# A second attention whose scores rotate over three PSUM banks and whose exponentials run in halves

## The chip, the cores and the metric

The kernel runs on one core of a Trainium2 chip. A core has five engines with queues of their own, which meet only at semaphores: TensorE (PE, its weight loads PEld), VectorE (DVE), ScalarE (ACT), GpSimd (POOL) and SyncE (SP). TensorE writes its results to PSUM, eight banks of 128 partitions by 512 floats; VectorE and ScalarE read them there. The metric is the device time of one launch in microseconds, the median of several runs.

## The reference

A small language model on 16 sequences of 128 tokens: embedding with a decaying memory and four MLP layers, a fast weight attention, a mixture of experts, then a second attention and a second mixture. The change touches the second attention alone:

```python
def _L1_attn_ref(x, Wqk, Wv, Wpos, bpos, Wproj, bproj, gating):    # x: (16, 128, 64), 8 heads of 8
    qk = (x @ Wqk.T).reshape(Bb, Nn, 2, Hh, hd)
    q = qk[:, :, 0].transpose(0, 2, 1, 3)
    k = qk[:, :, 1].transpose(0, 2, 1, 3)
    patch_score = softmax(einsum('bhnd,bhmd->bhnm', q, k) * hd ** (-0.5))
    pos_score = softmax((rel @ Wpos.T + bpos).transpose(2, 0, 1))
    g = sigmoid(gating)[None, :, None, None]
    attn = (1.0 - g) * patch_score + g * pos_score[None]
    attn = attn / attn.sum(axis=-1, keepdims=True)
    v = (x @ Wv.T).reshape(Bb, Nn, Hh, hd).transpose(0, 2, 1, 3)
    out = einsum('bhnm,bhmd->bhnd', attn, v).transpose(0, 2, 1, 3).reshape(Bb, Nn, Cc)
    return out @ Wproj.T + bproj
h = h + _L1_attn_ref(_layernorm(h), ...)
h = h + _L1_ffn_ref(_layernorm(h), ...)
```

## The kernel before

Each engine has one program, written out by hand in the order in which it runs, and counts on named semaphores. The word token stands here for one of the T = 16 sequences (128 positions on the partitions); CH = 4 tokens make a chunk, and there are NC = 4 chunks. In the second attention a token's eight heads give scores of 128 x 1024, in two halves of four heads, 512 columns each, one PSUM bank a half. The semaphores are `s_mm0` and `s_mm1` (scores of a half), `s_sub` (maximum subtracted, two per token), `s_exp` (exponential), `s_T` (transposed, two per token), `p_ready` (copied to SBUF, two per token), `av_mm` (values multiplied).

TensorE, for each token t: `scores(t + 1)` (lines 1759 to 1772, sixteen products of 64 rows, into banks 2 and 3), after both halves of token t have been subtracted; at odd t `values_back` (line 1806); `values(t - 1)` (line 1793); side work by the place j of the token in its chunk: j = 0 `turn_input` of the next chunk (line 1816) and, in odd chunks, `positional` (line 1840); j = 1 `project_qk` (lines 1825 and 1826); j = 3 `turn_attended` (line 1850) and `project_v` (line 1831); then `turn_scores(t)` (line 1781, eight transposes into banks 4 and 5); at j = 3 `project_out` (line 1856).

VectorE, for each token: `normalise(t)` (lines 2488 to 2499), for each half the maximum out of PSUM (line 2494) and the subtraction from PSUM to the SBUF tile `sexp` (line 2498); behind it side work: layer norms (lines 409 to 424), `mix` (lines 2508 to 2515), `add_attended` (line 2521).

ScalarE, for each token: `take_turned(t - 1)`, two copies of 512 columns from banks 4 and 5 to `pexp` (line 1226); one exponential over the token's 1024 columns in `sexp` (line 1243); side work: j = 0 `save_values_T` (line 1218) and `take_x` (line 1185), in odd chunks `take_positions` (line 1210); j = 1 two query copies (line 1190) and the keys (line 1195) of the next chunk; j = 2 `save_values_T` and the other two query copies; j = 3 `take_attended` (line 1204) and `take_values` (line 1199).

`sexp` and `pexp` hold two tokens each. Scores of the first token of a chunk wait for that chunk's four query copies. Behind the last token TensorE goes on with `turn_x` (line 1640) for the second mixture of experts. GpSimd works out the layer norms' factors (lines 391 to 402) and adds to `H`; no DMA runs in this stretch.

Of the kernel before, what the change touches and what calls it, by code (L numbers as in the profile page):

```python
# [6 lines left out]
ACT = mybir.ActivationFunctionType  # L7
# [5 lines left out]
P = 128  # L13


T = 16
# [3 lines left out]
D = 64  # L20
# [3 lines left out]
HD = D // NH  # L24
# [114 lines left out]
def build(nc, a):  # L139
# [9 lines left out]
    with ExitStack() as ctx:  # L149
        def sb(name, shape, dt=F32):  # L150
            return ctx.enter_context(nc.sbuf_tensor(name, shape, dt))
# [4 lines left out]
        bank = [ctx.enter_context(nc.psum_tensor(f"bank{i}", [P, 512], F32)) for i in range(8)]  # L156
# [4 lines left out]
        ident = sb("ident", [P, P])  # L161
# [108 lines left out]
        sexp = KKf[:, 0:2048].rearrange("p (k h n) -> p k h n", k=2, h=NH)  # L270
        pexp = UVf[:, 4608:6656].rearrange("p (k h n) -> p k h n", k=2, h=NH)
# [94 lines left out]
        def turn_bank(k, c):  # L366

            return bank[6 if k == 0 else 2 + c if c < 2 else c % 2]

        def expert_bank(k, c, e):  # L370

# [511 lines left out]
        def _(act):  # L883
# [313 lines left out]
            def take_values(c):  # L1197
                act.wait_ge(s["d_v"], c + 1)
                act.activation(vaug[c % 2][:, :, :, 0:HD], bank[1][:, 0:CH * D].rearrange("p (t h d) -> p t h d", t=CH, h=NH),
                               ACT.Copy).then_inc(s["d_vcopy"], 1)  # L1200
# [16 lines left out]
                    act.wait_ge(s["av_back"], p - 1)  # L1217
                act.activation(avT[:, p % 2, :], bank[6][:], ACT.Copy).then_inc(s["av_saved"], 1)

            def take_turned(t):  # L1220

                for g in range(2):
                    act.wait_ge(s["s_T"], 2 * t + g + 1)
                    if t >= 2:
                        act.wait_ge(s["av_mm"], t - 1)
                    act.activation(pexp[:, t % 2, 4 * g:4 * g + 4, :].rearrange("p h n -> p (h n)"), bank[4 + g][:],
                                   ACT.Copy).then_inc(s["p_ready"], 1)

            save_sums(2)
            take_x(0)  # L1230
# [4 lines left out]
            take_values(0)  # L1235
            for t in range(T):
                c, j = divmod(t, CH)
                if t:
                    take_turned(t - 1)
                if t == T - 1:  # L1240
                    take_attended(NC - 2)
                act.wait_ge(s["s_sub"], 2 * t + 2)
                act.activation(sexp[:, t % 2], sexp[:, t % 2], ACT.Exp, scale=float(HD) ** -0.5).then_inc(s["s_exp"], 1)

                if t and t % 2 == 0:
                    save_values_T(t // 2 - 1)
                if j == 0 and c % 2:
                    take_positions(c // 2)
                if j == 3 and c and t < T - 1:
                    take_attended(c - 1)  # L1250
                if c + 1 < NC:
                    if j == 0:
                        take_x(c + 1)
                    elif j == 1:
                        queries(c + 1, 0, 2)
                        take_keys(c + 1)
                    elif j == 2:
                        queries(c + 1, 2, NH // 2)
                    else:
                        take_values(c + 1)  # L1260
            def save_weights(h):
                act.wait_ge(s["wT_mm"], 1 + h)
                r = slice(D * h, D * h + D)
                act.activation(wtsT[r, :], bank[6][r, 0:P], ACT.Copy).then_inc(s["wT_ready"], 1)

            def router_tanh(h):
                act.wait_ge(s["rl_arg"], 1 + h)
                r = rsel[:, 8 * h:8 * h + 8, :]
                act.activation(r, r, ACT.Tanh).then_inc(s["rl_tanh"], 1)

            take_turned(T - 1)
            experts(1, 0)
            save_values_T(T // 2 - 1)
            experts(1, 1)
# [16 lines left out]
        def _(pe):  # L1291
            mm = nc.tensor.matmul
# [294 lines left out]
            for k in range(2):  # L1587
                for j in range(4):
                    last = nc.tensor.transpose(bank[k][:, P * j:P * j + P], plog[:, 4 * k + j, :], ident[:])
# [37 lines left out]
            tr = nc.tensor.transpose  # L1627
# [131 lines left out]
            def scores(t):  # L1759

                n = slice(P * (t % CH), P * (t % CH) + P)
                q_, k_ = qd[t // CH % 2], kz[t // CH % 2]
                if t % CH == 0:
                    pe.wait_ge(s["d_qd"], NH // 2 * (t // CH + 1))
                    pe.wait_ge(s["d_kcopy"], t // CH + 1)
                if t:
                    pe.wait_ge(s["s_sub"], 2 * t)
                for j in range(NH // 2):
                    low = mm(bank[2][:, P * j:P * j + P], q_[0:D, j, n], k_[0:D, n], start=True, stop=True)  # L1769
                    high = mm(bank[3][:, P * j:P * j + P], q_[D:P, j, n], k_[D:P, n], start=True, stop=True)  # L1770
                low.then_inc(s["s_mm0"], 1)
                high.then_inc(s["s_mm1"], 1)

            def turn_scores(t):

                pe.wait_ge(s["s_exp"], t + 1)
                for g in range(2):
                    if t:
                        pe.wait_ge(s["p_ready"], 2 * (t - 1) + g + 1)
                    for j in range(4):  # L1780
                        last = tr(bank[4 + g][:, P * j:P * j + P], sexp[:, t % 2, 4 * g + j, :], ident[:])
                    last.then_inc(s["s_T"], 1)

            def values(t):
                pe.wait_ge(s["p_ready"], 2 * t + 2)
# [82 lines left out]
            for t in range(T):  # L1868
                c, j = divmod(t, CH)
                if t + 1 < T:  # L1870
                    scores(t + 1)
                if t % 2 and t > 2:
                    values_back(t // 2 - 1)
                if t:
                    values(t - 1)
                if t == T - 1:
                    turn_attended(NC - 2)
                if j == 0 and c % 2:
                    positional(c // 2)
                if j == 0 and c + 1 < NC:  # L1880
                    turn_input(c + 1)
                if j == 1 and c + 1 < NC:
                    project_qk(c + 1)
                if j == 3 and c and t < T - 1:
                    turn_attended(c - 1)
                if j == 3 and c + 1 < NC:
                    project_v(c + 1)
                turn_scores(t)
                if j == 3 and c:
                    project_out(c - 1)  # L1890
            def router(c):
# [66 lines left out]
        def _(dve):  # L1958
# [529 lines left out]
            def normalise(t):  # L2488

                for g in range(2):  # L2490
                    x = bank[2 + g][:].rearrange("p (h m) -> p h m", h=4)
                    m = smax[:, t % 2, 4 * g:4 * g + 4]
                    dve.wait_ge(s[f"s_mm{g}"], t + 1)
                    ch(dve.tensor_reduce(m, x, AX_X, ALU.max))
                    if t >= 2 and g == 0:
                        dve.wait_ge(s["s_T"], 2 * (t - 1))
                    ch.settle()
                    tt(sexp[:, t % 2, 4 * g:4 * g + 4, :], x, m.unsqueeze(2).broadcast_to([P, 4, P]), sub)\
                        .then_inc(s["s_sub"], 1)
# [32 lines left out]
            for t in range(T):  # L2532
                c, j = divmod(t, CH)
# [157 lines left out]
```

## Time and profile before

| | us |
|---|---|
| median of three runs (618.89 to 621.03) | 619.0 |
| the profiled execution, whole | 620.1 |
| its span, first to last instruction | 618.3 |
| TensorE busy in the span | 545.9 |
| VectorE busy | 427.9 |
| ScalarE busy | 357.5 |
| GpSimd busy | 346.6 |
| TensorE's mean granted clock, as a share of full speed | 0.982 |

The page of the profile is an overview of one execution. Its chain of work that ended last, followed back from the last instruction, lies on TensorE for 50% of the span and on VectorE for 21%. The timeline lists instructions in order of time, neighbours of one kind merged; the number in brackets is the idle time of the engine before the row and the instruction that ended it. A wait for several semaphores is put down to the one that came last by the profile. TensorE's busy time is that of pipelined products, and starts are more exact than ends.

### The profile page before, as it was taken

What the parts mean: (1) busy time and instruction counts of PE and PEld (TensorE: products, weight loads), DVE (VectorE), ACT (ScalarE), POOL (GpSimd) and SP (SyncE); (2) the same over time, 40 slices, a digit from 0 to 9 for tenths busy, and PEclk for the clock granted to TensorE, in tenths of its full rate; (3) what the DMA queues carried; (4) which work ended last, traced back from release to release, by engine and by line L of the source; (5) the groups of instructions that cost most, each with busy time, mean ns of one, the idle gap of its engine ahead of it and who ended that gap; (6) DMA issues with size and microseconds to landing.
All of it is one profiled execution on the core that took longest, in us unless ns stands there. A gap on an engine that the chain in (4) does not pass through costs nothing.

```text
span 618.3 us, 12438 instructions
## 1 busy us (share of the span) xinstructions
PE 545.9 (88%) x4494; PEld 415.2 (67%) x4494; DVE 427.9 (69%) x1088; ACT 357.5 (58%) x949; POOL 346.6 (56%) x474
## 2 busy tenths in 40 slices
PE   7989999999987786777888888898999898989996
PEld 3556767778434675556777777786577676765785
DVE  4953563423887787699989988899425987766444
ACT  1264444444676674224768878774596667767430
POOL 2597653311360776788999899998466320001445
PEclk9999999999999988899999999998999899999998
DMA  8000000000000434300000000000000000000000
GB/s 280 16 2 1 2 0 1 1 1 1 1 1 2 72 79 74 80 0 2 2 1 1 1 2 2 1 1 1 2 2 2 0 3 1 2 2 1 9 9 18
DMA packets 10860, 10.43 MB, mean 17 GB/s; under 512 B 6000, under 2 KB 9840, under 8 KB 10544
## 3 DMA queue, kind: packets, MB, share of 16 engines
q1 hardware_dynamic: 8080, 7.54, 4.5%
q0 software_dynamic: 2144, 1.75, 1.5%
q8 instruction: 36, 0.59, 0.4%
q10 hardware_dynamic: 576, 0.35, 0.2%
q14 instruction: 24, 0.20, 0.1%
HBM read 5.77 MB, written 0.52 MB: 10 GB/s over the span
## 4 chain that ended last, share of the span: by engine, by line
PE 50%; DVE 21%; POOL 9%; ACT 7%; DMA 5%; issue 5%; SPq 2%; DVEq 0%; POOLq 0%; ACTq 0%
PE bank L1355 8%; PE bank L1343 7%; PE bank L1442 6%; PE bank L1658 5%; PE bank L1724 5%; DVE bank L2174 3%; PE bank L1616 3%; DVE features L2168 2%; PE bank L1721 2%; SPq L460 2%; POOL features L600 2%; PE bank L1769 2%; DVE features L2144 2%; DMA coefs<-G 1%; POOL rstd L393 1%
## 5 line engine op out<-in xcount | busy, mean ns | idle before, releaser
L1442 PE MATMUL bank<-ident,features 128*128 128x128 f32 x604 | 77.9, 279 | 12.2 <-DVE features L2144 9.3
L1442 PEld LDWEIGHTS bank<-ident,features 128*128 128x128 f32 x604 | 68.5, 145 | 19.9 <-DVE features L2144 15.2
L909 ACT ACTIVATE G<-bank,cols 128x512 f32<-128x512 f32 x64 | 43.9, 686 | 53.0 <-PE bank L1343 53.0
L600 POOL TENSOR_TENSOR features<-UV,coefs 128x1024 f32<-128x1024 f32 (+3 forms) x36 | 59.6, 1671 | 3.6 <-DVE UV L2131 3.6
L1355 PE MATMUL bank<-weights,G 128*128 128x128 f32 x512 | 59.9, 275 | 0.0
L1343 PE MATMUL bank<-xs,weights 128*128 128x512 f32 x128 | 57.8, 594 | 0.9 <-ACT xs L900 0.9
L1355 PEld LDWEIGHTS bank<-weights,G 128*128 128x128 f32 x512 | 58.5, 192 | 0.0
L2144 DVE TENSOR_TENSOR features<-UV,bank 128x1024 f32<-128x1024 f32 (+3 forms) x68 | 55.7, 863 | 0.7 <-ACT bank L992 0.2
L400 POOL TENSOR_SCALAR rstd<-mv 128x4 f32<-128x4 f32 x8 | 1.6, 194 | 91.0 <-DVE mv L412 91.0
L999 ACT ACTIVATE xs<-UV,coefs 128x32 f32<-128x32 f32 x232 | 50.3, 308 | 0.0
L999 ACT ACTIVATE sx<-UV,coefs 128x32 f32<-128x32 f32 x200 | 43.5, 308 | 0.0
L573 POOL TENSOR_TENSOR UV<-xs,rows 128x512 f32<-128x512 f32 x16 | 20.2, 1267 | 38.7 <-DVE xs L2033 38.6
L2174 DVE TENSOR_REDUCE bank<-features 128x32 f32<-128x1024 f32 (+3 forms) x40 | 41.0, 1051 | 0.0
L1433 PE MATMUL bank<-features 32*128 32x136 f32 x768 | 32.5, 300 | 8.5 <-DVE G L2092 1.9
L1343 PEld LDWEIGHTS bank<-xs,weights 128*128 128x128 f32 x128 | 23.1, 190 | 25.0 <-issue 22.7
L1616 PE MATMUL bank<-RK,ident 128*128 128x256 f32 x160 | 38.6, 390 | 0.0
L424 DVE TENSOR_SCALAR UV<-xs,mv,rstd 128x128 f32<-128x128 f32 x52 | 20.8, 463 | 24.9 <-POOL rstd L393 23.2
L1433 PEld LDWEIGHTS bank<-features 32*128 32x128 f32 x768 | 27.2, 195 | 13.9 <-issue 4.8
L393 POOL TENSOR_TENSOR rstd<-rstd,neghalf 128x4 f32<-128x4 f32 x32 | 33.4, 1044 | 2.7
L2033 DVE TENSOR_TENSOR xs<-bank,UV 128x512 f32<-128x512 f32 x16 | 11.1, 691 | 33.2 <-PE bank L1355 31.2
L1616 PEld LDWEIGHTS bank<-RK,ident 128*128 128x128 f32 x160 | 30.3, 198 | 3.7
L2168 DVE TENSOR_TENSOR features<-RK,bank 128x1024 f32<-128x1024 f32 (+3 forms) x32 | 32.2, 1007 | 0.7
(362 smaller groups left out, 1350.2 us busy)
## 6 DMA issues: line engine op xcount, KB each, us to landing
weights<-in_w SPq DMA_DIRECT2D x2, 1024.0 KB, 9.8
features<-in_tok SPq DMA_DIRECT2D x1, 768.0 KB, 5.8
weights<-in_ew SPq DMA_DIRECT2D x4, 128.0 KB, 3.5
weights<-in_ew SPq DMA_DIRECT2D x2, 256.0 KB, 3.3
coefs<-G POOLq DMA_DIRECT2D x16, 25.5 KB, 4.4
rows<-in_rows SPq DMA_DIRECT2D x1, 384.0 KB, 6.4
out_h<-H SPq DMA_DIRECT2D x3, 128.0 KB, 2.0
coefs<-G SPq DMA_DIRECT2D x14, 25.5 KB, 4.3
```

What stands on the lines that cost most here:

```text
L393: pool.tensor_tensor(rstd[:, k, 0:n], rstd[:, k, 0:n], neghalf[:, 0:n], ALU.pow).then_inc(s["ln_rstd"], 1)
L600: pool.tensor_tensor(out, u, co, ALU.mult).then_inc(s["held_p"], 1)
L909: act.activation(G[:, 4 * (w % 2) + f, :], up_bank(f)[:], ACT.Gelu, bias=col("b1", 4 * i + f)).then_inc(s["tok_gelu"], 1)
L999: last = act.activation(own[t % 2][:, k, DH * h:DH * h + DH], UV[:, FIRST[t] + k, 0, DH * h:DH * h + DH], ACT.Copy, scale=C[:, t, 2 * NH + ...
L1343: mm(up_bank(f)[:], w1[:, i, P * f:P * f + P], xT[:, w % 2, :], start=True, stop=True).then_inc(s["tok_up"], 1)
L1355: last = mm(down_bank(w)[:, DT * j:DT * j + DT], G[:, 4 * (w % 2) + f, P * j:P * j + P], w2[:, i, f, :], start=(f == 0), stop=(f == 3))
L1433: last = mm(bank[4 * k + j][:, GB * SL * n:GB * SL * n + GB * SL], feat[left + k][x, g, 0:T].rearrange("p s b -> p (s b)"), feat[right + k ...
L1442: last = mm(out[:, P * k:P * k + P], x[:, P * k:P * k + P], ident[:], is_transpose=True, start=first and k == 0, stop=last_ and k == n - 1 ...
L1616: mm(bank[1][:, HB:2 * HB], ident[:], RK[:, 0, :], start=True, stop=True)
L2144: dve.tensor_tensor(out, u, co.unsqueeze(3).broadcast_to([P, R, NH, DH]), ALU.mult)\
L2168: ch(dve.tensor_tensor(PD[:, j, 0:R * HB].rearrange("p (r x) -> p r x", r=R), RK[:, r0:r1_, :], e.unsqueeze(1).broadcast_to([P, R, HB]), A ...
L2174: ch(dve.tensor_reduce(bankCR[:, r0:r1_, :], PD[:, j, 0:(r1_ - r0) * HB].rearrange("p (r h j) -> p r h j", r=r1_ - r0, h=NH), AX_X, ALU.add))
```

## The change

The halves of the scores, numbered 2t + g, go to banks 2, 3 and 5 in turn. `scores(t + 1)` wait for the first half of token t only, since that is the last reader of the banks that they write. All turned exponentials go to bank 4, so a half's transposes wait for the copy of the half before. The exponential runs in two calls of 512 columns, one for each half. On TensorE the transposes of the first half stand right behind `scores(t + 1)`, ahead of `values_back` and `values(t - 1)`; those of the second half stay where both stood. On ScalarE the order within token t is exponential of half 0, copy of half 0, exponential of half 1, side work, copy of half 1; before, it was both copies of token t - 1, exponential of t, side work. VectorE's program is the same but for the banks that it reads.

```diff
--- before.py
+++ after.py
@@ -366,6 +366,10 @@
         def turn_bank(k, c):
 
             return bank[6 if k == 0 else 2 + c if c < 2 else c % 2]
+
+        def score_bank(n):
+
+            return bank[(2, 3, 5)[n % 3]]
 
         def expert_bank(k, c, e):
 
@@ -1217,14 +1221,19 @@
                     act.wait_ge(s["av_back"], p - 1)
                 act.activation(avT[:, p % 2, :], bank[6][:], ACT.Copy).then_inc(s["av_saved"], 1)
 
-            def take_turned(t):
-
-                for g in range(2):
-                    act.wait_ge(s["s_T"], 2 * t + g + 1)
-                    if t >= 2:
-                        act.wait_ge(s["av_mm"], t - 1)
-                    act.activation(pexp[:, t % 2, 4 * g:4 * g + 4, :].rearrange("p h n -> p (h n)"), bank[4 + g][:],
-                                   ACT.Copy).then_inc(s["p_ready"], 1)
+            def exponential(t, g):
+
+                act.wait_ge(s["s_sub"], 2 * t + g + 1)
+                x = sexp[:, t % 2, 4 * g:4 * g + 4, :]
+                act.activation(x, x, ACT.Exp, scale=float(HD) ** -0.5).then_inc(s["s_exp"], 1)
+
+            def take_turned(t, g):
+
+                act.wait_ge(s["s_T"], 2 * t + g + 1)
+                if t >= 2:
+                    act.wait_ge(s["av_mm"], t - 1)
+                act.activation(pexp[:, t % 2, 4 * g:4 * g + 4, :].rearrange("p h n -> p (h n)"), bank[4][:],
+                               ACT.Copy).then_inc(s["p_ready"], 1)
 
             save_sums(2)
             take_x(0)
@@ -1235,13 +1244,11 @@
             take_values(0)
             for t in range(T):
                 c, j = divmod(t, CH)
-                if t:
-                    take_turned(t - 1)
+                exponential(t, 0)
+                take_turned(t, 0)
+                exponential(t, 1)
                 if t == T - 1:
                     take_attended(NC - 2)
-                act.wait_ge(s["s_sub"], 2 * t + 2)
-                act.activation(sexp[:, t % 2], sexp[:, t % 2], ACT.Exp, scale=float(HD) ** -0.5).then_inc(s["s_exp"], 1)
-
                 if t and t % 2 == 0:
                     save_values_T(t // 2 - 1)
                 if j == 0 and c % 2:
@@ -1258,6 +1265,8 @@
                         queries(c + 1, 2, NH // 2)
                     else:
                         take_values(c + 1)
+                take_turned(t, 1)
+
             def save_weights(h):
                 act.wait_ge(s["wT_mm"], 1 + h)
                 r = slice(D * h, D * h + D)
@@ -1268,7 +1277,6 @@
                 r = rsel[:, 8 * h:8 * h + 8, :]
                 act.activation(r, r, ACT.Tanh).then_inc(s["rl_tanh"], 1)
 
-            take_turned(T - 1)
             experts(1, 0)
             save_values_T(T // 2 - 1)
             experts(1, 1)
@@ -1764,22 +1772,21 @@
                     pe.wait_ge(s["d_qd"], NH // 2 * (t // CH + 1))
                     pe.wait_ge(s["d_kcopy"], t // CH + 1)
                 if t:
-                    pe.wait_ge(s["s_sub"], 2 * t)
+                    pe.wait_ge(s["s_sub"], 2 * t - 1)
                 for j in range(NH // 2):
-                    low = mm(bank[2][:, P * j:P * j + P], q_[0:D, j, n], k_[0:D, n], start=True, stop=True)
-                    high = mm(bank[3][:, P * j:P * j + P], q_[D:P, j, n], k_[D:P, n], start=True, stop=True)
+                    low = mm(score_bank(2 * t)[:, P * j:P * j + P], q_[0:D, j, n], k_[0:D, n], start=True, stop=True)
+                    high = mm(score_bank(2 * t + 1)[:, P * j:P * j + P], q_[D:P, j, n], k_[D:P, n], start=True, stop=True)
                 low.then_inc(s["s_mm0"], 1)
                 high.then_inc(s["s_mm1"], 1)
 
-            def turn_scores(t):
-
-                pe.wait_ge(s["s_exp"], t + 1)
-                for g in range(2):
-                    if t:
-                        pe.wait_ge(s["p_ready"], 2 * (t - 1) + g + 1)
-                    for j in range(4):
-                        last = tr(bank[4 + g][:, P * j:P * j + P], sexp[:, t % 2, 4 * g + j, :], ident[:])
-                    last.then_inc(s["s_T"], 1)
+            def turn_scores(t, g):
+
+                pe.wait_ge(s["s_exp"], 2 * t + g + 1)
+                if t or g:
+                    pe.wait_ge(s["p_ready"], 2 * t + g)
+                for j in range(4):
+                    last = tr(bank[4][:, P * j:P * j + P], sexp[:, t % 2, 4 * g + j, :], ident[:])
+                last.then_inc(s["s_T"], 1)
 
             def values(t):
                 pe.wait_ge(s["p_ready"], 2 * t + 2)
@@ -1869,6 +1876,7 @@
                 c, j = divmod(t, CH)
                 if t + 1 < T:
                     scores(t + 1)
+                turn_scores(t, 0)
                 if t % 2 and t > 2:
                     values_back(t // 2 - 1)
                 if t:
@@ -1885,7 +1893,7 @@
                     turn_attended(c - 1)
                 if j == 3 and c + 1 < NC:
                     project_v(c + 1)
-                turn_scores(t)
+                turn_scores(t, 1)
                 if j == 3 and c:
                     project_out(c - 1)
             def router(c):
@@ -2488,7 +2496,7 @@
             def normalise(t):
 
                 for g in range(2):
-                    x = bank[2 + g][:].rearrange("p (h m) -> p h m", h=4)
+                    x = score_bank(2 * t + g)[:].rearrange("p (h m) -> p h m", h=4)
                     m = smax[:, t % 2, 4 * g:4 * g + 4]
                     dve.wait_ge(s[f"s_mm{g}"], t + 1)
                     ch(dve.tensor_reduce(m, x, AX_X, ALU.max))
```

## Rows read from the trace of the kernel before

**Rows 1.** The page: busy time, share of the span and instructions of each engine.
```profile
PE 545.9 (88%) x4494; PEld 415.2 (67%) x4494; DVE 427.9 (69%) x1088; ACT 357.5 (58%) x949; POOL 346.6 (56%) x474
```

**Rows 2.** Timeline: first scores, scores of the last token, next stage (start, us, engine).
```profile
478.85 0.37 PE L1769 MATMUL bank<-features 64*128 64x128 f32 x1
...
546.10 0.37 PE L1769 MATMUL bank<-coefs 64*128 64x128 f32 x1 [0.71 <-DVE features L2498]
...
554.20 1.04 PE L1640 MATMUL bank<-ident,xs 128*128 128x128 f32 x8
```

**Rows 3.** The second attention: us; busy PE, PEld, DVE, ACT, POOL; clock, DMA, GB/s.
```profile
478.80:555.20 76.40, 66.06 (x792) 53.69 (x791) 59.81 (x151) 52.23 (x84) 12.15 (x20) 0.98 0.01 2
```

**Rows 4.** Waits of TensorE in that stretch: us in total, times, longest.
```profile
PE bank L1769 <- DVE features L2498: 4.6, 5, 1.4
...
PE bank L1781 <- ACT features L1243: 2.5, 4, 1.6
...
PE bank L1793 <- ACT UV L1226: 2.0, 4, 0.7
```

**Rows 5.** Timeline, tokens 5 to 7: TensorE and ScalarE alone, [idle before <-releaser].
```profile
504.93 0.37 PE L1769 MATMUL bank<-coefs 64*128 64x128 f32 x1
...
506.02 0.66 PE L1806 MATMUL bank<-picked,UV 128*128 128x128 f32 x4
...
506.61 0.64 PE L1793 MATMUL bank<-UV,coefs 128*32 128x128 f32 x16
...
507.18 0.69 PE L1825 MATMUL bank<-sx,weights 64*128 64x512 f32 x1
...
508.24 1.09 PE L1781 MATMUL bank<-ident,features 128*128 128x128 f32 x8
...
508.34 1.26 ACT L1190 ACTIVATE features<-bank,m 128x512 f32<-128x512 f32 x2 [1.62 <-PE bank L1825]
...
509.26 0.18 PEld L1769 LDWEIGHTS bank<-coefs 64*128 64x128 f32 x1 [0.17 <-issue]
...
509.50 0.60 ACT L1195 ACTIVATE features<-bank 128x512 f32<-128x512 f32 x1
...
509.97 1.09 ACT L1226 ACTIVATE UV<-bank 128x512 f32<-128x512 f32 x2
...
510.93 1.08 ACT L1243 ACTIVATE features<-features 128x1024 f32<-128x1024 f32 x1
...
511.88 0.62 ACT L1218 ACTIVATE UV<-bank 128x512 f32<-128x512 f32 x1
...
512.07 1.09 PE L1781 MATMUL bank<-ident,features 128*128 128x128 f32 x8 [0.30 <-ACT features L1243]
...
512.35 1.30 ACT L1190 ACTIVATE features<-bank,m 128x512 f32<-128x512 f32 x2
...
513.71 0.37 PE L1769 MATMUL bank<-features 64*128 64x128 f32 x1 [0.55 <-ACT features L1190]
```

**Rows 6.** Timeline, token 13: a group of transposes and the copies behind it.
```profile
544.29 1.09 PE L1781 MATMUL bank<-ident,features 128*128 128x128 f32 x8
...
544.99 1.09 ACT L1226 ACTIVATE UV<-bank 128x512 f32<-128x512 f32 x2 [1.21 <-PE bank L1781]
```

**Rows 7.** Timeline, start of the stretch: both subtractions of token 0, scores of token 1.
```profile
480.83 0.69 DVE L2498 TENSOR_TENSOR features<-bank,RK 128x512 f32<-128x512 f32 x1
...
482.16 0.69 DVE L2498 TENSOR_TENSOR features<-bank,RK 128x512 f32<-128x512 f32 x1
...
482.90 0.37 PE L1769 MATMUL bank<-features 64*128 64x128 f32 x1 [1.43 <-DVE features L2498]
```

**Rows 8.** Busy time in three stretches; the number behind POOL is the granted clock.
```profile
480.20:483.60 3.40, 1.97 (x22) 1.78 (x23) 3.33 (x8) 1.16 (x2) 1.39 (x3) 1.00 0.00 0
...
483.60:487.00 3.40, 3.40 (x22) 2.86 (x18) 2.85 (x6) 1.53 (x3) 0.64 (x1) 0.51 0.00 0
...
548.50:551.90 3.40, 2.00 (x28) 1.29 (x26) 1.64 (x3) 2.11 (x5) 0.00 (x0) 1.00 0.02 7
```

## The prediction, made before the changed kernel ran

> **What bounds the kernel now.** I read the page first: TensorE is busy 88% of the span, VectorE 69%, ScalarE 58% [rows 1]. The second attention is the stretch from the first scores at 478.85 us to the transposes of the next stage at 554.20 us, 75.4 us for sixteen tokens [rows 2]. In its busy table TensorE works 66.06 us of 76.40, VectorE 59.81, ScalarE 52.23 [rows 3]. So there are 10.3 us of idle TensorE to win at most, and no engine has much room. The waits view tells whom TensorE waited for: VectorE's subtraction of the maximum in front of the scores (4.6 us), ScalarE's exponential in front of the transposes (2.5 us), ScalarE's copies in front of the values (2.0 us) [rows 4]. Then I read the timeline token by token, since each token carries another piece of side work (j is the token's place in its chunk of four).
>
> The slots come from there, each the distance between two starts on one engine. On TensorE from token 5 to 6 [rows 5]: scores 1.09 us (504.93 to 506.02), values_back 0.59, values 0.57, project_qk 1.06, eight transposes with the change of tile form behind them 1.02, of which 0.17 is that change, so four transposes 0.44. On ScalarE [rows 5]: two query copies 1.16 (508.34 to 509.50), keys 0.47, two turned copies 0.96, an exponential over 1024 columns 0.95, save_values 0.47. Delays: project_qk's start to the first query copy 1.16; the last copy or exponential to TensorE 0.06 (510.93 + 1.08 to 512.07); start of a group of transposes to ScalarE's copy 0.70 [rows 6]; subtraction's start to the scores 0.74 (482.16 to 482.90) [rows 7].
>
> **Scores over three banks.** Scores(t+1) now wait for the first half of token t's subtraction alone. For token 1 that is 480.83 + 0.74 = 481.57 in place of 482.90, so 1.33 us are gained at the start [rows 7]. Later the loop from scores to scores over VectorE shrinks by the second half, 1.3 us (480.83 to 482.16), and VectorE, with 59.81 us of work, ceases to release the scores. All of the 4.6 us of waiting goes, as far as nothing else comes late. What is late next is ScalarE, as follows.
>
> **Turned exponentials in one bank, exponentials in halves.** The arithmetic is the same: 32 exponentials of 512 columns for 16 of 1024. No row shows a 512 column Exp. Its bounds are half of a 1024 column slot, 0.47, and the 0.60 that a single copy of 512 lasts (two overlapping ones last 1.09 [rows 5]); I take a slot of 0.49 and a result for TensorE 0.65 after its start, since exponential (0.95 for 1024) and two copies (0.96 for 2 x 512) run at the same pace. So the work grows by under 0.1 us a token; below nothing it can't go, the columns being the same. The order does more. ScalarE now runs exponential(t,0), copy(t,0), exponential(t,1), side work, copy(t,1). Between the first two lies a round trip: exponential 0.65, transposes to copy 0.70, so the copy starts 1.35 us after the exponential, of which ScalarE works 0.49. It stands idle for 0.86 us in each token in which TensorE was already waiting, with the whole queue behind it. And transposes(t,0) sit ahead of values(t-1) on TensorE, so TensorE waits with them for exponential(t,0), which waits behind copy(t-1,1), which stands behind the side work of token t-1. Formerly values(t-1) filled that gap.
>
> Tokens 5 to 8 show it. Before: the query copies start at 508.34, and the same engine, fully busy, reaches the next two at 512.35, 4.01 us later; they end at 513.65 and release scores(8) at 513.71 [rows 5]. After: 1.16 queries, 0.47 keys, 0.49 copy, 1.35 until copy(6,0), 0.49, 0.49 for exponential(6,1), 0.47 save_values, make 4.92. The distance from scores(7) to scores(8) then becomes, with TensorE's own slots: ready at 0; scores 1.09; transposes wait until 2.26 (queries were 0.51 before zero, plus 1.16, 0.48, 0.49 and 0.65); the query copies start at 4.41, end at 5.69, scores(8) at 5.73. It was 4.45 [rows 5]. This costs 1.28 us. It recurs from scores(11) to (12), 1.30 us, and from scores(3) to (4), 0.93 us.
>
> **The sum.** I wrote both halves of each token on in this way for TensorE, ScalarE and VectorE, with the same slots, side by side with the sixteen starts of before (first and last in [rows 2], the fourteen between in the same view). Change of each distance, in us: up to scores(1) -1.33; to (2) -0.48, (3) 0, (4) +0.93, (5) +0.14, (6) +0.39, (7) +0.20, (8) +1.28, (9) 0, (10) -0.78, (11) +0.26, (12) +1.30, (13) 0, (14) +0.24, (15) -0.38; from there to 554.20 +0.55. The negative ones are tokens in which VectorE released the scores; the zeros at (9) and (13) are TensorE at work without a wait, where nothing can be had. +0.14 to +0.39 are mostly one more change of tile form (0.17, transposes(t,0) to values) at tokens without values_back, and the wait of transposes(t,1). The last one: after token 14 there are no scores left to cover copy(14,1) to exponential(15,0), some 1.4 us of idle TensorE, of which 0.9 was there before. Together +2.3 us. At scores(4) the forecast is still 0.9 us ahead; it falls behind at scores(8).
>
> Behind the stage TensorE is on the chain without long waits, its instructions in the old order, so the 2.3 us pass through. Nothing is moved on the DMA queues or GpSimd. The profiled execution took 620.1 us for a span of 618.3, 1.8 around it, and gives 620.1 + 2.3 = 622.4; it lay 1.1 over the median of 619.0. On the median the forecast is 619.0 + 2.3 = 621.3 us.
>
> **Where the slots can be off.** The half exponential enters twice in a token; at 0.47 or 0.60 it moves the sum by -0.4 or +2.0 us (twice 0.02 or 0.11 in some nine tokens that ScalarE binds). The change of tile form at eight tokens costs between 0 and 1.4, I took 0.17 each. Own range of the forecast: 619.5 to 623.5.
>
> **The clock.** Between 480.2 and 483.6 TensorE was busy 1.97 us of 3.40; in the next 3.40 us it was granted 0.51, nearly 1.2 GHz instead of 2.4 GHz [rows 8]. My sum assumes full clock throughout, since the idle time at 481.5 shrinks to 0.3 us. But the new order makes emptier stretches of its own: at tokens 6 and 10, 1.18 and 0.66 and 1.0 us idle within 4.7 us, and at tokens 14 to 15 0.66 and 1.4 us within 2.5 us. Against it speaks 548.5 to 551.9, busy 2.00 of 3.40 too and followed by a clock of 1.00 [rows 8]. The Trainium skill, TensorE: Matmul & The Clock Gate, section "A second HAM failure mode: psum-queue depth-cycling", tells of a kernel that cycled through PSUM banks and whose short idles made the clock swing. By that rule the extra stalls here would be paid for a second time, and this is the second rival; the trace agrees in one of the two stretches.
>
> **The rivals.** First, faster. The halves overlap as they are meant to, the round trip lies under side work of ScalarE, and only the waits for VectorE count: 619.0 - 4.6 [rows 4] + 8 x 0.17 = 615.8 us. It would need the side work to stand between exponential and copy; the code has it behind exponential(t,1) in every token. The Trainium skill, Perfetto Trace Analysis, section "Optimizing Scalar/DVE Operations", advises this cut where an unsaturated ScalarE causes bubbles on another engine: "breaking up instructions may allow work to be completed sooner". It decides if ScalarE's idle time beside its 52.23 us doesn't grow. Second, slower: the clock falls after one or two of the new stalls; 3.4 us at half speed lose 1.7 us of TensorE's work, and token 7, 11 or the next stage has no idle time to absorb it. One gives 623.0, two 624.7; I price it at 623.9. It decides from one such stretch on. Third, the change does little of what it says: early scores only move TensorE's wait from in front of the scores to in front of the transposes, and the late copy costs less than I think because TensorE's side work of tokens 1, 5 and 9 covers it; then 619 within 1 us.
>
> **How the numbers follow.** Forecast 50% (of it a fifth beyond 622.1), clock 28%, overlap 12%, no effect 10%. 0.5% is 3.1 us, about what a measurement can tell from no change. Faster by more (under 615.9): 0.11, from the overlap. Slower by more (over 622.1): 0.10 + 0.26 = 0.36. Within: 0.53. The range goes from 618.0, below the third rival's middle, to 625.0, above two clock losses; it leaves out the overlap and worse clock losses, under 2 in 10.
>
> **What would show it.** Scores(1) near 481.6; no wait for VectorE in front of scores over 0.3 us; ScalarE idle about 0.8 us between its first exponential and the first copy of most tokens; TensorE idle about 1.2 us ahead of the first transposes of tokens 2, 6 and 10; more than 1 us ahead of those of token 15; scores(8) 5.7 us after scores(7). Wrong would be: ScalarE's busy time in the stage more than 2 us off 52, a copy less than 1.2 us behind its exponential, or a half speed stretch in the stage.

## The result and the profile after

The changed kernel took 626.19 us (median of six runs, 623.51 to 627.38), the kernel before beside it 620.82: a ratio of 1.0082, interval 1.0050 to 1.0113. It is slower by some 5 us, where 2.3 were forecast, and its time lies above the range.

The second attention is where the time went. From its first scores to `turn_x` it took 75.35 us before [rows 2] and takes 80.72; the part behind it takes 64.14 us in both. The first scores start at 480.03 in place of 478.85, but nothing was changed ahead of them: in four profiles of the kernel before they start between 477.99 and 480.47. So I compare the length of this stretch alone, and below I call it the stage. The only DMA in it is of instructions, 9 packets before and after, and no wait of TensorE is put down to them. Here is its row, which answers to [rows 3], and the waits in it, which answer to [rows 4], first TensorE's, then ScalarE's:

```profile
480.03:560.75 80.72, 68.78 (x779) 53.48 (x779) 58.74 (x147) 54.33 (x99) 12.13 (x20) 0.96 0.01 2
...
PE bank L1788 <- ACT features L1228: 7.9, 12, 1.2
PE bank L1777 <- ACT coefs L1194: 2.0, 2, 1.0
PE bank L1777 <- ACT features L1194: 1.0, 1, 1.0
...
ACT UV L1235 <- PE bank L1788: 15.9, 19, 1.5
```

Scores (now line 1777) wait for VectorE (line 2506) nowhere; 4.6 us of such waits are gone. In their place the transposes (line 1788) wait 7.9 us for an exponential (line 1228), formerly 2.5, and the copies (line 1235) stand 15.9 us on ScalarE for transposes, formerly 2.5. Tokens 5 to 7 show how, beside [rows 5] (other rows between these are left out):

```profile
509.76 1.26 ACT L1194 ACTIVATE features<-bank,m 128x512 f32<-128x512 f32 x2 [0.95 <-PE bank L1832]
510.24 0.37 PE L1777 MATMUL bank<-coefs 64*128 64x128 f32 x1
510.91 0.60 ACT L1199 ACTIVATE features<-bank 128x512 f32<-128x512 f32 x1
511.39 0.61 ACT L1235 ACTIVATE UV<-bank 128x512 f32<-128x512 f32 x1
511.87 0.65 ACT L1228 ACTIVATE features<-features 128x512 f32<-128x512 f32 x1
512.57 0.66 PE L1788 MATMUL bank<-ident,features 128*128 128x128 f32 x4 [1.16 <-ACT features L1228]
513.26 0.60 ACT L1235 ACTIVATE UV<-bank 128x512 f32<-128x512 f32 x1 [0.75 <-PE bank L1788]
513.75 0.62 ACT L1228 ACTIVATE features<-features 128x512 f32<-128x512 f32 x1
514.27 0.59 ACT L1222 ACTIVATE UV<-bank 128x512 f32<-128x512 f32 x1
514.43 0.66 PE L1788 MATMUL bank<-ident,features 128*128 128x128 f32 x4 [0.63 <-ACT features L1228]
514.75 1.27 ACT L1194 ACTIVATE features<-bank,m 128x512 f32<-128x512 f32 x2
516.07 0.37 PE L1777 MATMUL bank<-features 64*128 64x128 f32 x1 [0.99 <-ACT features L1194]
```

Half g of token t is written (t, g). Copy(5,1) runs at 511.39, behind queries and keys; exponential(6,0) at 511.87; the transposes at 512.57; copy(6,0) at 513.26. ScalarE's chain from query copies to query copies is 514.75 - 509.76 = 4.99 us, forecast 4.92, before 4.01. And there is something that the sum had left out, the granted clock (the third number from the end):

```profile
532.00:535.40 3.40, 1.83 (x24) 1.15 (x24) 1.59 (x3) 2.76 (x6) 0.00 (x0) 1.00 0.00 0
535.40:539.60 4.20, 4.15 (x40) 3.27 (x40) 2.58 (x4) 2.12 (x4) 0.00 (x0) 0.60 0.00 0
552.00:556.50 4.50, 2.62 (x31) 1.95 (x32) 2.98 (x5) 2.76 (x6) 0.00 (x0) 1.00 0.01 2
556.50:561.00 4.50, 4.50 (x39) 3.56 (x38) 0.05 (x1) 2.26 (x4) 0.00 (x0) 0.62 0.02 4
```

Behind the stalls of token 10, and again behind those of 14 and 15, the clock fell to 1.2 GHz for a while, both times where TensorE has next to no idle time left (busy 4.15 us of 4.20, and 4.50 of 4.50).

The distances between the starts of the scores put both together. They are worked out from the timeline of each kernel, in us; the last is from scores(15) to `turn_x`. Half clock means 1.2 GHz in place of 2.4; an asterisk marks a distance that is longer by it. The forecast row is the row of before with the changes of the sum added.

| to | (1) | (2) | (3) | (4) | (5) | (6) | (7) | (8) | (9) | (10) | (11) | (12) | (13) | (14) | (15) | end | stage |
|---|---|---|---|---|---|---|---|---|---|---|---|---|---|---|---|---|---|
| before | 4.05 | 4.25* | 4.09 | 4.61 | 4.17 | 4.91 | 4.33 | 4.45 | 5.37 | 4.34 | 4.33 | 4.44 | 5.38 | 4.47 | 4.06 | 8.10 | 75.35 |
| forecast | 2.72 | 3.77 | 4.09 | 5.54 | 4.31 | 5.30 | 4.53 | 5.73 | 5.37 | 3.56 | 4.59 | 5.74 | 5.38 | 4.71 | 3.68 | 8.65 | 77.67 |
| after | 2.73 | 3.67 | 4.08 | 5.71 | 4.16 | 5.25 | 4.61 | 5.83 | 5.37 | 3.54 | 4.64 | 5.83 | 6.93* | 4.62 | 3.77 | 9.98* | 80.72 |

Fourteen of sixteen are within 0.2 us of the forecast. The other two are 1.55 and 1.33 above it. One of the prediction's own signs of being wrong shows here beside the half speed stretch: ScalarE's busy time in the stage is 54.33 us, 2.3 over its 52. With the halves alone, put into the kernel before (below), it is 53.20 for 51.80, so some 1.4 us come with the halves; the rest I take to be calls that stand alone where they ran overlapped before, which no run shows by itself.

### The profile page after: what moved, and what is told of

Same layout as the page of the kernel before. It is cut to its first block, busy times and chain, and to the rows that moved or that the text cites. A ratio compares the mean times of both kernels' runs of the same rounds, so it can differ in the third digit from the quotient of the medians.

```text
span 624.9 us, 12470 instructions
## 1 busy us (share of the span) xinstructions
PE 551.0 (88%) x4494; PEld 416.4 (67%) x4494; DVE 427.9 (68%) x1088; ACT 360.7 (58%) x965; POOL 347.0 (56%) x474
## 4 chain that ended last, share of the span: by engine, by line
PE 33%; DVE 13%; ACT 6%; POOL 5%; issue 4%; POOLq 0%; DVEq 0%; ACTq 0%
PE bank L1450 6%; PE bank L1666 5%; PE bank L1732 5%; DVE bank L2182 3%; PE bank L1624 2%; DVE features L2176 2%; PE bank L1788 2%; PE bank L1729 2%; POOL features L604 2%; DVE features L2152 2%; POOL features L624 1%; ACT features L1228 1%; PE bank L1777 1%; PE bank L1800 1%; PE bank L1506 1%
## 5 line engine op out<-in xcount | busy, mean ns | idle before, releaser
L1450 PE MATMUL bank<-ident,features 128*128 128x128 f32 x604 | 76.6, 275 | 11.3 <-DVE features L2152 8.1
L1450 PEld LDWEIGHTS bank<-ident,features 128*128 128x128 f32 x604 | 66.7, 142 | 19.6 <-DVE features L2152 14.5
L1441 PE MATMUL bank<-features 32*128 32x136 f32 x768 | 35.7, 326 | 10.3 <-issue 5.8
L1441 PEld LDWEIGHTS bank<-features 32*128 32x128 f32 x768 | 30.7, 218 | 15.4 <-issue 9.1
L1624 PE MATMUL bank<-RK,ident 128*128 128x256 f32 x160 | 37.2, 379 | 0.0
```

The lines of the kernel that those rows point to most:

```text
L1441: last = mm(bank[4 * k + j][:, GB * SL * n:GB * SL * n + GB * SL], feat[left + k][x, g, 0:T].rearrange("p s b -> p (s b)"), feat[right + k ...
L1450: last = mm(out[:, P * k:P * k + P], x[:, P * k:P * k + P], ident[:], is_transpose=True, start=first and k == 0, stop=last_ and k == n - 1 ...
L1624: mm(bank[1][:, HB:2 * HB], ident[:], RK[:, 0, :], start=True, stop=True)
```

## The experiments

Stage lengths come from one profile of each kernel, unless more are named; where a distance repeats without half clock it does so within 0.03 us, so a stage is measured more sharply than a whole run, whose times spread over some 5 us. Ratios are of whole runs against the kernel before.

**The changed kernel and the kernel before, again.**

> The changed kernel once more, for a second profile. If its stalls bring the half clock: one to three half clock stretches in the second attention again, stage 79 to 82 us. If it is chance: none, stage 77.8 us. The other distances within 0.1 us of the first profile in either case.

> The changed kernel, third profile. Distances at full clock as in the first two within 0.05 us; if the stalls bring the half clock, again two or three stretches in the second attention, stage 80.5 to 82.5 us.

> The kernel before once more. Stage 75.1 us without a half clock stretch; with one early in it, as in the first profile, 75.4. If the clock falls by chance, as likely to have one as the changed kernel.

> The kernel before, third profile: stage 75.04 us without a half clock stretch, 75.3 with one at the start. If the half clock belongs to the changed order, no more than one stretch; if it is chance, two or three as often as in the changed kernel.

> The same, fourth profile: 75.04 to 75.4 us, at most one stretch, if the half clock belongs to the changed order.

The changed kernel's stage took 82.14 and 82.02 us, with half clock from the end of distance (4) through (5) (6.68 and 6.59 for 4.17) and in (9) (6.97 for 5.37): a spell twice as long as the others behind token 2 and one behind token 6, each behind a stall of the same kind. Their whole runs took 626.51 and 625.47 us. Before: 75.07, 75.08 and 75.74, half clock in the last alone, at the start of the stage as in [rows 8]; whole runs 618.95, 621.46 and 620.46. Joining the undisturbed distances of the three profiles gives the changed kernel at full clock: 78.0 us, against 75.07. The rows are those of the second profile of the changed kernel, around token 2, and its whole stage, then the stage of the kernel before in its second profile:

```profile
489.00:493.30 4.30, 2.63 (x39) 2.01 (x40) 4.13 (x16) 3.55 (x8) 1.08 (x2) 1.00 0.00 0
493.30:500.40 7.10, 6.29 (x49) 4.92 (x47) 5.88 (x19) 3.43 (x7) 2.15 (x4) 0.52 0.01 3
...
478.48:560.62 82.14, 70.14 (x780) 54.75 (x779) 58.75 (x147) 54.22 (x99) 12.12 (x20) 0.94 0.01 1
...
477.99:553.06 75.07, 63.45 (x779) 51.53 (x779) 58.98 (x147) 51.81 (x83) 12.13 (x20) 1.00 0.01 2
```

So the stage is 3.0 us longer at full clock, and 2.7 to 4.1 more come with the half clock in these profiles, where the kernel before loses 0 to 0.7 to it. Together that is 5.4 to 7 us, at and above the 5.1 of the whole runs.

**Do the stalls bring the half clock?** First with four dummy products, whose result nobody reads, ahead of each wait for an exponential:

```diff
+                    pe.wait_ge(s["p_ready"], 2 * t + g)
+                    for _ in range(4):
+                        mm(bank[4][:, 0:P], ident[:], ident[:], start=True, stop=True)
                 pe.wait_ge(s["s_exp"], 2 * t + g + 1)
```

> The changed kernel with four dummy products (0.44 us) into bank 4 ahead of each of TensorE's waits for an exponential half, so that its stalls are shorter but nothing comes earlier. If the stalls of the new order bring the half clock: no granted clock under 1.00 in the second attention, the stage at 77.8 to 79 us in place of 80.72. If half clock falls there by chance or by what ran before: it is there as often as in the changed kernel, and the stage takes 79 to 82 us.

No half clock, but the stage took 96.82 us where 77.8 to 79 were expected, and the ratio is 1.0303. I had priced a dummy like a transpose, 0.11 us; it takes 0.27, four filled more than the wait, and at most of the 31 places TensorE wasn't waiting (12 such waits in the stage of the changed kernel). Filled so far over its waits, the kernel says little on the cause. Then two dummies, only where TensorE waits in any case:

```diff
+                if t % 4 == 2 or (t, g) == (T - 1, 0):
+                    for _ in range(2):
+                        mm(bank[4][:, 0:P], ident[:], ident[:], start=True, stop=True)
                 pe.wait_ge(s["s_exp"], 2 * t + g + 1)
```

> The changed kernel with two dummy products (0.43 us) behind the wait for bank 4 and ahead of the wait for the exponential, and only at tokens 2, 6, 10, 14 (both halves) and 15 (first half), where TensorE waits 0.49 us or more at that very place. Nothing useful comes earlier or later: the distances without a half clock stretch stay within 0.1 us. If the emptiness of these tokens is what brings the half clock: none or one stretch in the second attention, stage 78.0 to 79.5 us, whole kernel about 3 us under the changed kernel. If not: two to three stretches, 80.5 to 82.

> The changed kernel with the few dummy products once more, second profile. If the emptiness of tokens 2, 6, 10 and 14 to 15 brings the half clock: none or one stretch in the second attention, stage 78.7 to 80.3 us, against two or more in all three profiles of the changed kernel. If the first profile was luck: two or three stretches, 81 to 83 us.

> The same, third profile: none or one stretch if the emptiness is the cause, two or three if it is not.

The stages took 78.77, 78.75 and 78.75 us, all three at full clock. The ratio of the first is 1.0058, interval 1.0030 to 1.0085, some 1.5 us under the changed kernel's 1.0082 where about 3 were expected; the two intervals overlap, so the whole runs alone don't tell the two kernels apart (the second and third profiled runs took 623.22 and 628.03 us). The first profile, around token 2: the dummies are line 1788, each leaving two records, the transposes 1791.

```profile
491.53 0.71 PE L1788 MATMUL bank<-ident 128*128 128x128 f32 x4 [0.64 <-ACT UV L1235]
492.08 0.63 PE L1791 MATMUL bank<-ident,features 128*128 128x128 f32 x4
...
495.55 0.37 PE L1777 MATMUL bank<-coefs 64*128 64x128 f32 x1 [0.99 <-ACT coefs L1194]
...
489.50:493.50 4.00, 3.25 (x44) 2.44 (x43) 3.83 (x17) 3.25 (x7) 0.75 (x3) 1.00 0.02 4
493.50:500.50 7.00, 6.01 (x74) 5.12 (x76) 6.56 (x19) 5.18 (x11) 2.72 (x4) 1.00 0.00 1
```

Two dummies take 0.55 us (491.53 to 492.08), not 0.43; (4), (15) and the end are 0.12, 0.12 and 0.30 longer than undisturbed, which is most of the 0.7 us over 78.0. Work that computes nothing took away all half clock in three profiles of three, where the changed kernel has two spells in each of three, and made the stage 2 to 3.4 us shorter. The other kernels below point the same way: of those made from the changed one, the two that keep its order on ScalarE (fourth and fifth) have two and three spells, the four with another order there (second, sixth, eighth and tenth) none, in one profile each. I take it as shown that these spells need the idle time of these tokens. Whether it counts that the idle time is shorter or that products were added isn't told apart. Nor does every empty stretch bring a fall: of the changed kernel's four places (tokens 2, 6, 10 and 14 to 15) two are hit in each profile. The kernel before has a stretch at its own end that is emptier than [rows 8] and kept full clock in four profiles of four; in the ninth kernel, whose end is the same, the clock fell behind it. What decides between them stays open. Their rows, the kernel before and then the ninth:

```profile
549.00:552.40 3.40, 1.50 (x23) 0.80 (x21) 1.14 (x2) 2.08 (x4) 0.00 (x0) 1.00 0.02 7
552.40:555.80 3.40, 3.37 (x41) 3.01 (x41) 1.33 (x9) 1.86 (x3) 0.00 (x0) 1.00 0.00 0
...
549.40:552.80 3.40, 1.47 (x23) 0.82 (x22) 1.03 (x2) 1.97 (x3) 0.00 (x0) 1.00 0.02 7
552.80:556.20 3.40, 3.40 (x18) 3.40 (x19) 0.15 (x1) 1.19 (x2) 0.00 (x0) 0.54 0.00 0
```

**The scores' early start.** The wait of before put back, `2 * t - 1` to `2 * t`:

```diff
-                    pe.wait_ge(s["s_sub"], 2 * t - 1)
+                    pe.wait_ge(s["s_sub"], 2 * t)
```

> The changed kernel with scores(t+1) waiting for both halves' subtraction, as before; all else as changed. This takes the early start away that three banks allow. My sum: distances in which VectorE releases the scores grow, (1) by 1.3, (2) by 0.4, (10) by 0.8, others little: stage 79.5 to 81 us at full clock, against 77.8. Rival (the early scores gain nothing because ScalarE is late anyway): 77.8 to 78.3.

84.73 us, with three half clock spells; with its three disturbed distances replaced by the undisturbed ones of the changed kernel about 80.4. The distances (1) 4.06, (2) 3.98, (10) 4.34 and (15) 4.05 are those of before. So the early start that three banks allow brings 2.4 us, as forecast; the ratio without it is 1.0161 (1.0121 to 1.0202).

**The exponential in halves, alone in the kernel before.**

```diff
+                for g in range(2):
+                    act.wait_ge(s["s_sub"], 2 * t + g + 1)
+                    x = sexp[:, t % 2, 4 * g:4 * g + 4, :]
+                    act.activation(x, x, ACT.Exp, scale=float(HD) ** -0.5).then_inc(s["s_exp"], 1)
```

> The kernel before with one part of the change: each token's exponential in two calls of 512 columns, back to back, and TensorE waits for each half; banks and orders as before. My schedule: two half calls take 0.98 us of ScalarE's queue for 0.95, and the first transposes can start 0.45 us earlier where TensorE waited for the exponential (four waits, 2.5 us). The second attention (75.35 us before) becomes 74.3 to 75.5. Rival (a half call costs its full 0.60 of the queue): +0.25 us in each token that ScalarE binds, 76 to 77.

74.92 us at full clock against 75.07; ratio 1.0014 (0.9982 to 1.0045). (8) and (12) are 0.09 longer, the end 0.35 shorter. From one half's start to the next call's it is 0.52 us, so two halves hold ScalarE's queue for 1.04 us where one call held it for 0.95; that is the 0.09. Two calls cost next to nothing, and gain as little.

**The round trip.** This is the way of a half from ScalarE's exponential over TensorE's transposes back to ScalarE's copy. ScalarE now runs exponential(t,0), exponential(t,1), copy(t,0):

```diff
                 exponential(t, 0)
-                take_turned(t, 0)
                 exponential(t, 1)
+                take_turned(t, 0)
```

> The changed kernel with ScalarE's order exponential(t,0), exponential(t,1), copy(t,0), side work, copy(t,1). My schedule: the round trip of 1.35 us is filled by the second exponential, ScalarE's idle time in it falls from 0.86 to 0.37 us, scores(7) to (8) from 5.83 to about 5.3, the stage from 77.8 (changed kernel without half clock) to between 74 and 75.5. Rival (the late copy(t,1) behind the side work is what costs, not the round trip): under 0.5 us gained, about 77.5. Half clock stretches add up to 1.5 us each in either.

The stage took 75.72 us at full clock, 2.3 less than 78.0; (4) and (8) came down from 5.71 and 5.83 to 5.24 and 5.43, and ScalarE's wait in front of the copies, 15.9 us after, is gone for two thirds. Its rows, the stage and that wait:

```profile
483.65:559.37 75.72, 65.22 (x779) 51.41 (x779) 58.66 (x147) 55.00 (x99) 12.11 (x20) 1.00 0.01 2
...
ACT UV L1235 <- PE bank L1788: 5.7, 15, 1.0
```

The ratio is 0.9994 (0.9973 to 1.0015). Moving one line gives back 2.3 of the 3.0 us lost at full clock, and there is no half clock in its one profile. The stage is 0.2 over my bounds for it. ScalarE runs the same 99 instructions in it, so their number isn't what changed.

**TensorE's order.** `turn_scores(t, 0)` moved behind `values_back` and `values(t - 1)`:

```diff
-                turn_scores(t, 0)
                 if t % 2 and t > 2:
                     values_back(t // 2 - 1)
                 if t:
                     values(t - 1)
+                turn_scores(t, 0)
```

> The changed kernel with the first half's transposes behind values_back and values(t-1), as before. My schedule: values (0.57 us) fill TensorE's wait for exponential(t,0), and one change of tile form (0.17) goes at eight tokens, but copy(t,0) starts 0.1 to 0.25 us later in tokens that ScalarE binds; the stage changes by -1.5 to 0 us from 77.8. Rival (TensorE's order is what costs): 75.5, the time of before.

83.55 us with half clock in (4), (5) and (9). Of the undisturbed distances some are shorter, (6) 4.87 for 5.25 and (14) 4.43 for 4.62, and others longer, (10) 4.12 for 3.54 and (15) 4.70 for 3.77. With (5) taken from the changed kernel and (9) from its own (13), 5.63, the stage at full clock is an estimated 79.2 us, over my bounds of 76.3 to 77.8 and far over the rival's 75.5: TensorE's place for these transposes isn't what costs; ratio 1.0126 (1.0079 to 1.0173).

**Other orders for the same banks.** The sixth kernel lets TensorE run transposes(t-1,1) behind scores(t+1), and ScalarE a whole exponential between the two copies, with the values saved late at j = 2 (ScalarE's part of the edit is left out here):

```diff
+                if t:
+                    turn_scores(t - 1, 1)
                 if t % 2 and t > 2:
                     values_back(t // 2 - 1)
...
-                turn_scores(t, 1)
+                turn_scores(t, 0)
```

> Three banks for scores and one for turned exponentials kept, the orders put so that no round trip stands alone: TensorE runs transposes(t-1,1) behind scores(t+1) and transposes(t,0) at the end of token t; ScalarE runs copy(t-1,0), the whole exponential(t), copy(t-1,1), side work, and saves the values behind the query copies at j = 2. My schedule: the waits for VectorE stay away (-1.3 at the start, -0.8 at token 10) and ScalarE's chain between the query copies is no longer than before: stage 72.5 to 74.5 us at full clock, 1 to 2.5 under the kernel before. Rival (one bank for both turned halves costs a round trip whatever the order): 76 to 78.

78.17 us at full clock, 3.7 over my bounds and just over the rival's, that one bank for both turned halves costs a round trip whatever the order; ratio 1.0048 (1.0018 to 1.0078). The wait moved once more: values(t-1) (line 1805) now stand behind copy(t-1,1), and transposes (line 1793) behind the copy that empties bank 4.

```profile
PE bank L1805 <- ACT UV L1235: 8.2, 15, 1.1
PE bank L1793 <- ACT UV L1235: 3.0, 4, 0.8
```

In the eighth and the tenth, made from the second, the values are saved behind the query copies at j = 2, and in the tenth behind copy(t,1) too; the ninth has the first of these moves in the kernel before:

```diff
-                if t and t % 2 == 0:
+                if t and t % 4 == 0:
                     save_values_T(t // 2 - 1)
...
+                if j == 2:
+                    save_values_T(t // 2 - 1)
```

> The kernel of the second experiment (both exponentials ahead of the first copy) with the saving of the values behind the query copies at j = 2, so that 0.47 us leave ScalarE's chain ahead of scores(4), (8) and (12). My schedule: (4), (8), (12) each 0.4 to 0.47 shorter than 5.24, 5.43, 5.43; stage 75.72 - 1.3 = 74.4 us, 0.6 under the kernel before. Rival (another wait stands right behind): over 75.3.

> The kernel before with that same move and nothing else. (8) and (12) were released by the query copies, 0.55 us late for TensorE: each 0.4 to 0.47 shorter; (4) was released by VectorE and stays. Stage 75.04 - 0.9 = 74.1 us. If it is under e8, three banks and halves bring nothing that a one line move does not.

> The kernel of the eighth run (both exponentials first, the values saved late) with the saving moved once more, behind copy(t,1) at j = 2. The eighth run gained 0.6 us at (8) and (12) and lost 0.4 at (5), (9) and (13), where the saving stood in front of copy(t,1). If that copy's lateness is what the 0.4 were: (5) 4.17, (9) and (13) 5.37 again, (4), (8) and (12) as in the eighth run, stage 75.09 - 1.2 = 73.9 us at full clock, 1.2 under the kernel before. If not: 75 to 75.7.

Eighth: 75.09 us; (4), (8) and (12) fell by 0.6 where 0.4 to 0.47 was forecast, but (5), (9) and (13) rose by 0.4; ratio 0.9983 (0.9958 to 1.0008), the lowest of all and not to be told from 1. Tenth: 75.58, the same distances but for the end, 8.88 for 8.39; ratio 1.0026 (1.0002 to 1.0049). So it isn't the saving's place in front of copy(t,1) that made (5), (9) and (13) longer. The traces show what does: the saving and copy(6,1) both stand in front of exponential(7,0), in either order, and it starts 5.60 us behind scores(7) in both kernels. Its transposes come 1.49 us behind scores(8), 1.09 in the second kernel, and TensorE waits for it (the first row is the eighth kernel, the second the tenth):

```profile
514.69 0.66 PE L1790 MATMUL bank<-ident,features 128*128 128x128 f32 x4 [0.33 <-ACT features L1228]
...
518.79 0.66 PE L1790 MATMUL bank<-ident,features 128*128 128x128 f32 x4 [0.33 <-ACT features L1228]
```

Ninth: (8) and (12) 4.15 for 4.45, a gain of 0.3 each where 0.4 to 0.47 was forecast. Its profile has half clock at the start and at the end (9.42 for 8.10), 76.00 in all; with undisturbed distances in their place it is about 74.5 at full clock, ratio 1.0008 (0.9977 to 1.0040). By that estimate it lies under the eighth kernel's 75.09, so in the stage at full clock three banks and halves bring nothing that this one move doesn't; whole runs don't tell the two apart.

## Why the prediction was wrong

- **The schedule held.** Scores(1) came 1.32 us early for 1.33; no scores wait for VectorE; the copy stands 1.39 us behind its exponential for 1.35; TensorE is idle 1.16 us ahead of the first transposes of token 6 for 1.18, 1.21 ahead of those of token 15 for more than 1; scores(8) come 5.83 us after scores(7) for 5.73. The second experiment shows that the round trip, with all that queues behind it, is 2.3 of the 3.0 us.
- **One term was small.** A half exponential's result reaches TensorE after 0.70 us (511.87 to 512.57), not 0.65, and its slot is 0.52 (513.75 to 514.27), not 0.49. The two make 0.07 of the 0.10 us by which (8) is over the forecast, and the same terms are in (4), (12) and the end. In all the stage is 78.0 us at full clock for 77.67, a small part of the error.
- **The step that failed is the clock.** "My sum assumes full clock throughout" was taken for the likeliest case, with 50%, and the half clock for a rival with 28%. It is no mishap here: behind the very stalls that the sum found at tokens 2, 6, 10 and 14 to 15 the clock fell in every profile, at two of the four places each time. They cost 2.7 to 4.1 us of the stage, where the sum has nothing. The rival's price of 1.7 us a spell was near (1.1 to 1.6 against undisturbed distances, the longer one behind token 2 2.4 to 2.5), and so was its count: two spells in each profile, one of them of double length in two. Its time, 623.9, is 4.9 over 619.0; measured are 5.4 in the medians and 5.1 by the ratio, with an interval of 3.1 to 7.0.
- **The weighing.** I set one stretch that was busy 2.00 us of 3.40 without a fall against one of 1.97 with a fall [rows 8] and took full clock as the rule. The new order has four such stretches in each run, and in three profiles of three two of them were followed by a fall; one stretch for and one against say little on the chance that none of four is. The Trainium skill, TensorE: Matmul & The Clock Gate, section "A second HAM failure mode: psum-queue depth-cycling", says that short idles between groups of products make the clock swing. It was taken for a rival; the runs agree with it in kind, since the longest single idle time in these tokens is 1.2 us.
- **The range** ended at 625.0, counted from a median of 619.0 of three runs; with the later runs that median is 620.82. On the ratio the changed kernel would be at 624.1, inside the range: that the measured time lies above it is as much the low median of the first three runs as the clock. The range had no term for a shift of that median.
- **The first rival** (halves overlap, 615.8) needed the exponentials side by side. Where they are (second experiment), the kernel reaches that of before and no more. The early scores' 2.4 us are spent elsewhere; I take it to be on the late second copy and the shared bank, which no run tells apart.

## What to carry to other kernels

Where two halves share a buffer and go around through another engine, put the second half's work ahead of the first half's return in that engine's queue; otherwise each trip is paid as idle time with all that is queued behind it. Here that avoided the loss, but none of these orders made the kernel faster than before beyond the noise. When a forecast finds new stalls on TensorE in front of dense work, price the clock with them as part of the likeliest case, not as a mishap. A stage whose distances repeat to 0.03 us is the place to compare, when whole runs spread by 5 us.

## What the runs showed of the hardware

- Short idle times of TensorE can be paid twice. In tokens with 1.2, 0.6 and 1.0 us of it the clock often fell to 1.2 GHz behind (six spells at twelve such places in three profiles), at 1.1 to 2.5 us each. With 0.55 us of it filled twice a token by products into a bank about to be overwritten, the clock stayed at 2.4 GHz in three profiles, and the stage was 2.0 to 3.4 us shorter for 0.7 us of extra work. An empty stretch is no certain sign: one busy 1.50 us of 3.40 was followed by full clock.
- Two dummy products of 128 x 128 floats take 0.55 us, four transposes of the same size 0.44: here a transpose costs 0.11, a product 0.27.
- A 512 column exponential from SBUF lasts 0.62 to 0.66 us, a copy of as many columns from PSUM 0.60. The next call starts 0.52 us behind the exponential and 0.48 to 0.49 behind the copy; a 1024 column exponential lasts 1.09 and holds the queue for 0.95.
